# A gated delta rule and six local attention layers on one core: input stage written out as one sequence, output stage moved into the next block

## What is computed

```python
xn = _layernorm(x)
x  = x + gated_delta(xn) + local_layers(xn)      # both read xn alone
# gated_delta, 6 heads, keys 128 wide, values 32 wide
q = conv_silu(xn @ q_w.T); k = conv_silu(xn @ k_w.T); v = conv_silu(xn @ v_w.T)
# per token: S = S*exp(g); S += k (v - k S) beta; o = q S      (q, k scaled to length one)
out = (rms_norm(o) * norm_weight * silu(xn @ g_w.T)) @ o_w.T
# local_layers, six times: h += attn(shift(h)) @ Wo ; h += ffn(shift(h))
```

## Time and profile before

| | before |
|---|---|
| median of 3 runs | 2648.12 us (2646.16 to 2655.34) |
| the profiled execution, own time | 2652.6 us |
| its span | 2650.8 us |
| delta inputs, loop and tail | 24.5 to 178.3 us |
| chunks | 178.3 to 523.6 us |
| delta outputs | 524.8 to 558.8 us |
| local layers' block begins | 560.1 us |

### The profile page before, as it was taken

The page is one execution under the profiler, slowest core; times in us unless marked ns, Lnnn a source line. Parts: engine busy times, 40 slices in busy tenths (PEclk is TensorE's granted clock), DMA queues, the critical chain, the costliest instruction groups (busy, mean ns, idle before and its releaser), DMA issues. The chain is left out here.

```text
span 2650.8 us, 101393 instructions
## 1 busy us (share of the span) xinstructions
PE 2397.2 (90%) x42655; PEld 1589.1 (60%) x42655; DVE 1882.7 (71%) x3765; ACT 1358.9 (51%) x2430; POOL 1557.3 (59%) x2926
## 2 busy tenths in 40 slices
PE   6856999769999999999999999999999997799976
PEld 1224888645666666666666666666666664345544
DVE  6853554337888888888888888888888883576615
ACT  4731332215666556666666666666666663245532
POOL 0024565238877787778777877787777772122330
PEclk9966999959999999999999999999999998889977
DMA  1001111031211122122212221222111110100000
GB/s 36 0 5 30 31 29 30 17 128 50 58 50 52 55 68 69 50 66 60 75 49 63 58 77 50 66 61 78 50 44 45 47 49 26 28 3 4 4 1 16
DMA packets 99663, 118.03 MB, mean 45 GB/s; under 512 B 41342, under 2 KB 57742, under 8 KB 98446
## 3 DMA queue, kind: packets, MB, share of 16 engines
q1 hardware_dynamic: 99214, 111.58, 15.4%
HBM read 29.47 MB, written 7.34 MB: 14 GB/s over the span
## 5 line engine op out<-in xcount | busy, mean ns | idle before, releaser
L1768 POOL TENSOR_TENSOR l_rot_a<-l_rot_a,l_rot_b 128x512 f32<-128x512 f32 x384 | 482.1, 1275 | 214.7 <-DVE l_rot_b L1617 214.5
L1255 PE MATMUL l_A<-l_wts,l_H 128*128 128x512 f32 x768 | 399.5, 603 | 16.5 <-DMA l_maskb<-in_l_mask 10.2
L1777 POOL TENSOR_TENSOR l_qk<-l_rot_a,l_rn 128x512 f32<-128x512 f32 x384 | 388.3, 1043 | 21.5 <-POOLq L1815 21.5
L1611 DVE TENSOR_TENSOR l_rot_a<-l_A,l_tab 128x512 f32<-128x512 f32 x384 | 259.2, 675 | 179.8 <-ACT l_sq L1484 159.1
L1490 ACT ACTIVATE l_pT<-l_T 128x512 f32<-128x512 f32 x192 | 106.6, 595 | 426.3 <-PE l_T L1301 426.3
L1484 ACT ACTIVATE l_sq<-l_A 128x512 f32<-128x512 f32 x384 | 229.2, 597 | 122.5 <-PE l_A L1255 120.1
L1617 DVE TENSOR_TENSOR l_rot_b<-l_A,l_tab 128x512 f32<-128x512 f32 x384 | 261.0, 680 | 0.0
L1621 DVE TENSOR_REDUCE l_ss<-l_sq 128x8 f32<-128x512 f32 x384 | 259.4, 676 | 0.0
L1354 PE MATMUL l_T<-ident,l_qk 128*128 128x128 f32 x1536 | 207.6, 278 | 18.5 <-POOL l_qk L1777 12.0
L1354 PEld LDWEIGHTS l_T<-ident,l_qk 128*128 128x128 f32 x1536 | 173.3, 141 | 83.1 <-issue 58.5
L1360 PEld LDWEIGHTS l_T<-l_oT,l_wts 128*128 128x128 f32 x1536 | 186.3, 192 | 30.8 <-issue 22.1
(11 more groups left out here) (357 smaller groups left out, 5154.6 us busy)
## 6 DMA issues: line engine op xcount, KB each, us to landing
l_vw<-l_vn SPq DMA_DIRECT2D x384, 128.0 KB
l_vw<-l_vn SPq DMA_DIRECT2D x360, 64.0 KB
l_wts<-in_l_wts SPq DMA_DIRECT2D x18, 650.0 KB, 5.0
c_lower_out<-c_amt SPq DMA_DIRECT2D x16, 384.0 KB, 3.2
l_tab<-in_l_tables SPq DMA_DIRECT2D x6, 1024.0 KB, 5.4
l_wts<-in_l_wts SPq DMA_DIRECT2D x6, 635.5 KB, 4.7
c_inv<-c_bx SPq DMA_DIRECT2D x96, 8.0 KB
result<-x SPq DMA_DIRECT2D x4, 256.0 KB
```

What stands on the lines that cost most here:

```text
L1255: pe.matmul(A[j % 2][:], cols(m), w_of(m)[:, C_QKV + 512 * j:C_QKV + 512 * j + 512], start=True, stop=True).then_inc(pq_done, 1)
L1611: dve.tensor_tensor(rot_a[p][:, j, :].rearrange("p (a d) -> p a d", d=DH), src.rearrange("p (a d) -> p a d", d=DH), table[:, a, t:t + 1, : ...
L1768: pool.tensor_tensor(rot_a[m % 2][:, j, :], rot_a[m % 2][:, j, :], rot_b[:, j, :], ALU.add).then_inc(rot_rdy, 1)
L1777: pool.tensor_tensor(qk[:, j, :].rearrange("p (a d) -> p a d", d=DH), rot_a[p][:, j, :].rearrange("p (a d) -> p a d", d=DH), rn[p][:, 8 * ...
```

## The change

Four functions are touched.

- `delta_inputs`: the loop over two sequences is written out as 28 blocks. Of the tail, the 16 small projections `rates` (12 columns, `d_small`) stand behind PE's first block, five of the eight gate pairs (`gates`) stand between blocks, the log decay chain is on POOL, DVE takes two reciprocals behind its block 3, and the first sequence's norms are turned and rooted while the second sequence is being made. The second sequence's roots are on DVE behind the loop. Constants and cleared buffers of the chunks are made here (`Kept`).
- `delta_chunks`: DVE begins with `sums(0)`; the memsets and the reduction are gone; POOL scales the gates chunk by chunk (`scale_gate`).
- `delta_outputs` is gone as a block. Its work stands in `local_layers`: ahead of PE's first projection, with `x` added on DVE in slot -1.
- `local_layers`: SP asks for the first two weight parts and the tables ahead of the other parts and of the mask, with semaphores of their own; `vw` is cleared on POOL; POOL makes the tables of layer 0 ahead of the slots and those of layer 1 in slots 2 to 5; `gl` and `u` lie in the gates' buffer.

```diff
@@ delta_inputs, tensor
+            for i in range(BLOCKS):
+                b, f = divmod(i, NBLK)
+                project(i)
+                if i == 0:
+                    rates()
+                if f >= 2:
+                    sum_squares(b, f - 2)
+                if i == NBLK:
+                    pe.wait_ge(ld_rdy, 1)
+                    turn_norms(0)
...
+                if i in Z_AT:
+                    gates(Z_AT[i])
+            pe.wait_ge(ssq_rdy[0], 1)
+            turn_norms(1)
+            pe.wait_ge(conv_rdy, BLOCKS - 1)
+            for q in range(Z_LOOP, Z_PAIRS):
+                gates(q)
@@ delta_inputs, scalar
+            last_tap(0)
+            act.wait_ge(ab_done, 1)
+            act.activation(zab[:].rearrange("p t h -> p (t h)"), zab_ps, ACT.Copy).then_inc(ab_rdy, 1)
+            last_tap(1)
+            act.activation(a_log[:], a_log[:], ACT.Exp)
+            act.wait_ge(gate_step, 4)
+            act.activation(beta[:], beta[:], ACT.Exp, scale=-1.0)
+            act.activation(e1[:], s1[:], ACT.Exp, scale=-1.0).then_inc(exp_rdy, 1)
@@ delta_inputs, vector
+                if i == 3:
+                    dve.wait_ge(gate_step, 6)
+                    dve.reciprocal(s2[:], s2[:])
+                    dve.reciprocal(beta[:], beta[:]).then_inc(inv_rdy, 1)
+                if i == NBLK + 2:
+                    keep_turned(0)
+            keep_turned(1)
+            dve.wait_ge(ssq_rdy[1], 1)
+            rsqrt(dve, roots_of(1), ssq[1][:], rs_tmp[1][:], 0.0, 1e-6, rinv_step[1], 0, tick["dve"])
@@ delta_chunks, vector and gpsimd
+            sums(0)
             dve.tensor_tensor(gain[:], beta[:], r_k, ALU.mult).then_inc(small_rdy, 1)
-            for b in range(BATCH):
-                dve.memset(state[b][:], 0.0)
...
-            pool.tensor_tensor(gates, gates, r_q, ALU.mult).then_inc(scaled, 1)
...
                 if has(s - 1):
+                    scale_gate(s - 1)
                     gated(s - 1)
@@ local_layers, sync
-            for part in range(4):
-                weights(0, part)
+            sp.dma_start(o_wo, dram["d_wo"]).then_inc(o_ld, 16)
...
+            weights(0, 0)
+            weights(0, 1)
             tables(0)
+            sp.dma_start(x[:], dram["x"].rearrange("(t p) d -> p t d", p=P)).then_inc(x_ld, 16)
+            weights(0, 2)
+            weights(0, 3)
@@ local_layers, tensor
+            def turn_delta(w):
+                if w >= 2:
+                    pe.wait_ge(o_oT_rdy, w - 1)
...
+            def project_delta(w):
+                if w == 0:
+                    pe.wait_ge(wo_rdy, len(VB))
+                pe.wait_ge(o_oT_rdy, w + 1)
...
             pe.wait_ge(h0_rdy, 9)
-            pe.wait_ge(const_ld, 16)
+            turn_delta(0)
+            turn_delta(1)
+            for w in range(OUT_UNITS):
+                project_delta(w)
@@ local_layers, project_v
+                if m == 0:
+                    pe.wait_ge(w_ld[0], w_need(0))
+                    pe.wait_ge(o_x_rdy, NT)
@@ local_layers, vector
+                if n == -1:
+                    dve.wait_ge(x_ld, 16)
+                    dve.wait_ge(rs_step, RSQRT_STEPS)
+                    for t in range(NT):
+                        add_delta(t)
@@ local_layers, gpsimd
-            for layer in range(2):
-                for a in range(4):
-                    table(layer, a)
+            for p in range(2):
+                last = pool.memset(vw[p][:], 0.0)
...
+            for a in range(4):
+                table(0, a)
...
-                if n >= NT and 2 <= t < 6 and layer < DEPTH:
+                if n >= 0 and 2 <= t < 6 and layer < DEPTH:
                     table(layer, t - 2)
```

More of the change, by code:

```diff
@@ L127, in _, with gated_delta @@
             act.wait_ge(xnT_rdy, NT // GT)
-def gated_delta(nc, x, xn, ident, identb, dram, load_inputs):
+@dataclass
+class Kept:
+    tri: object
+    causal: object
+    blocks: object
+    second: object
+    eye: object
+    state: list
+    invT: list
+    u4: object
+    xd: object
+    upper: object
+def gated_delta(nc, x, xn, gate, ident, identb, dram, load_inputs):
     with ExitStack() as ctx:
@@ L136, in gated_delta @@
         vT = sb("vT", [P, len(VB), BATCH * SEQ])
-        gate = sb("gate", [P, NT, VD])
         beta = sb("beta", [P, NT, GH])
@@ L188, with delta_inputs @@
 SERIES = range(15, 1, -2)
-GATE_G = 13 + len(SERIES)
+W_LOADS = 16 * 9
 AMT = 4
 WIDE = 4
-def delta_inputs(nc, ident, xnT, qT, kT, vT, gate, beta, rinv, decay, weights):
+def delta_inputs(nc, ident, xnT, qT, kT, vT, gate, beta, rinv, decay, weights, kept):
     beta, logdecay = beta
@@ L340, in _, with last_tap @@
-            act.wait_ge(gate_step, 3)
-            act.activation(e1[:], s1[:], ACT.Exp, scale=-1.0).then_inc(act_step, 1)
+            def last_tap(i):
+                b, f = divmod(i, NBLK)
+                m = rows(f)
+                act.wait_ge(proj_done, i + 1)
+                if i >= 2:
+                    act.wait_ge(silu_rdy, i - 1)
+                act.activation(conv[i % 2][0:m, :], proj[i % 2][0:m, :], ACT.Copy, scale=w_conv[0:m, f, KCONV - 1:KCONV])\
+                   .then_inc(raw_rdy, 1)
@@ new lines, in keep_gates, with keep_norms @@
+            def keep_gates(q):
+                act.wait_ge(z_done, q + 1)
+                act.activation(gate[:, 2 * q:2 * q + 2, :].rearrange("p t d -> p (t d)"), gate_bank(q)[:, 0:2 * VD], ACT.Silu)\
+                   .then_inc(z_rdy, 1)
+            def keep_norms(b):
+                act.wait_ge(norm_done, 2 * GH * (b + 1))
+                for c in range(2):
+                    last = act.activation(ssqT[:, b, 512 * c:512 * c + 512], norms[c][0:2 * GH, :], ACT.Copy)
+                last.then_inc(norm_rdy, 1)
@@ L342, in _ @@
+            for q in range(Z_LOOP, Z_PAIRS):
+                keep_gates(q)
             act.wait_ge(sums_done, 1)
-            act.activation(decay[:].rearrange("p a t h -> p (a t h)"), sums[:, 0:3 * SMALL], ACT.Exp).then_inc(act_step, 1)
-            act.wait_ge(act_step, 4)
+            act.wait_ge(ssq_rdy[1], 1)
+            act.activation(decay[:].rearrange("p a t h -> p (a t h)"), sums, ACT.Exp).then_inc(decay_rdy, 1)
+            act.wait_ge(decay_rdy, 1)
+            act.wait_ge(z_rdy, Z_PAIRS)
@@ L409, in _ @@
[L409 to L419 removed]
+            pool.wait_ge(w_ld, W_LOADS)
@@ new lines, in _ @@
+            rsqrt(pool, roots_of(0), ssq[0][:], rs_tmp[0][:], 0.0, 1e-6, rinv_step[0], 0, tick["pool"])
+            pool.wait_ge(rinv_step[0], RSQRT_STEPS)
+            pool.tensor_scalar(rinv[:, 0:GH, 0:TB], rinv[:, 0:GH, 0:TB], float(HK) ** -0.5, None, ALU.mult).then_inc(rinv_rdy, 1)
+            for buffer in (*kept.state, *kept.invT, kept.u4, kept.xd, kept.upper):
+                last = pool.memset(buffer[:], 0.0)
+            last.then_inc(cleared, 1)
+            pool.wait_ge(cleared, 1)
@@ L421, in delta_chunks @@
+def delta_chunks(nc, spare, ident, identb, kqT, vT, gate, beta, logdecay, rinv, decay, kept, dram):
     with ExitStack() as ctx:
         sb, ps, sem = buffers(nc, ctx)
-        tri = sb("c_tri", [P, 3, P])
-        causal = sb("c_causal", [P, P], BF16)
-        blocks = sb("c_blocks", [P, P], BF16)
-        second = sb("c_second", [P, 2])
+        tri, causal, second, eye = kept.tri, kept.causal, kept.second, kept.eye
+        state, invT, u4, xd, upper = kept.state, kept.invT, kept.u4, kept.xd, kept.upper
```

502 lines of the change are left out of this document (235 added, 267 removed).

## The result

| | before | changed |
|---|---|---|
| median, same chip | 2649.63 us (2646.16 to 2655.34, 4 runs) | 2604.48 us (2600.08 to 2610.83, 4 runs) |
| the profiled execution, own time / span | 2652.6 / 2650.8 us | 2605.12 / 2603.4 us |

The ratio is 0.9829, 95% interval 0.9802 to 0.9857: 45 us faster. The forecast was 2613 us, with a range of 2594 to 2627. Borders are starts of instructions, and for the loop its end; the maximum (`l_mx`) is the first step of a tile's softmax on DVE, and the last column is the forecast's term for the stretch.

A forecast was written before the change was run, and what follows sets the result against it. It took DVE to bound the inputs' loop and PE at half clock the outputs, with waits at stage borders. Terms -9.7 - 10.7 - 17.8 - 1.3 + 4.2 = -35.3 us gave 2613 us, range 2594 to 2627.

The forecast's parts named there:

- its own case: Main forecast for the whole kernel, given 58%: 2604 to 2623 us, inputs gaining 4 to 18, tables costing 0 to 4.9.
- signs of being wrong: Full clock in the outputs, DVE taps idling in the loop after block 4, or chunks of another period than before.
- Loop's start: Inputs' loop, first blocks: small projections, ACT's exponentials, PE's line and reciprocals together cost +14.3 us, from +7 to +17.
- as PE is at half here I take 9: Inputs' loop behind block 0: the 32 small passes take 9 us on PE, between bounds of 3.9 and 11.5.
- Now ACT also loads the exponential's table: Inputs' loop before DVE's block 2: an added table load and three small exponentials on ACT cost 1.28 + 0.7 us.
- Border: Inputs' loop between the two sequences: DVE's idle time there goes, -6.6 us, less 0.3 for a copy.
- Tail: Behind the inputs' loop: 6.8 us of DVE work and a 2.0 us barrier replace 26.5 us, -17.7.
- chunks' setup: Start of the chunks' block: `sums(0)` comes first, so the first product waits 1.1 us instead of 11.9, -10.7.
- outputs: Output products at half clock within the local layers' block, transfers hidden behind PE: first rotary step 17.8 us sooner.
- roots: Local layers' start: POOL's roots follow the last rotated half after about 8.5 us instead of 9.9, -1.3.
- Tables: Layer 1's four tables in slots 2 to 5, where POOL is the bound: +4.2 us.
- The rival at the full clock: Outputs keep the full clock and take 11 us instead of 27.7: 17 us less, 2596 us; chance 20%.

The follow-up runs named there:

- The experiment on the rates: Changed kernel with the 32 small passes moved on PE behind block 2, ACT's copy and exponentials behind blocks 2 and 3, reciprocals behind block 6: 2605.68 us, ratio 0.9851.
- the side-by-side kernels: On one chip: the changed kernel as it is, 2603.99 us, and the same with spare transposes at two places in the local layers' block, 2591.91 us.
- the kernel with two fills: Changed kernel plus ten unread PE transposes behind the turned xn and ten behind the first two output turns, none at the chunks' end: 2591.91 us, ratio 0.9782.
- the one with tile 0 between the outputs: Changed kernel with tile 0's four local products and ACT's squares placed between the last five of eight output units: 2591.19 us, ratio 0.9798.
- the kernel before with fills: Kernel before plus ten spare transposes at the chunks' end and 32 in place of PE's wait for the output weights: 2638.06 us, ratio 0.995.

## Why the prediction was right, point by point

The number was right, and by luck as well as by its argument. Of the forecast's three steps for the loop, the start was off by 7.3 us and the pace by 5.4 in one direction, the border by 8.3 in the other, so that the loop's end came out within 4.6. And the median of 2604.48 lies at the edge of the 2604 to 2623 that the forecast gave its own case. One of its own signs of being wrong came true: DVE's taps idle in the loop behind block 4, at blocks 15 and 16. Of the other signs, block 2 stood at 39.9 and not at 50, the loop's end at 155 and not at 160, and the chunks' block at 163 and not at 169.

**Loop's start: mis-sized.** The step "as PE is at half here I take 9" priced the small projections. They took 3.87 us in the first profile, most of it at the full clock, and 6.84 at half: the bound of 11.5, from passes with 128 columns moving, doesn't hold for these with 12. The step "Now ACT also loads the exponential's table" was false: there is no such load in the trace, the changed kernel has fewer loads than before, and block 2 starts 4.9 us behind block 1, not 7.1. Nor does the one load take longer than its 1.28 us, as the next activation starts 0.01 us behind it. On the other side, from block 2 to block 4 it took 14.8 us and not the 12.0 of the forecast. Block 4 stood 7.0 us later, and 6.6 to 9.9 in nine profiles with this start, not 14.3. The experiment on the rates shows that pricing single passes was the wrong kind of sum: the idle time is shared among blocks 1 to 5.

**Loop's pace: a term that was missing.** The semaphore increments, in the diff for all to see, were not priced. 84 times 0.074 us are 6.2 us, shown by putting them back.

**Border: the step failed.** "At the border of the sequences the loop no longer drains", priced at -6.6. DVE's waits of 6.6 us went, but others of 8.3 came, as the work moved there stood ahead of the product that DVE waited for. The forecast had looked at the queue of the engine that gives the work up, not at the one that takes it. Moving it by two blocks and more gave 6.8 us against this profile, 5.7 on average. The half clock at that place is a part of it that the forecast had not reckoned with either.

**Tail, chunks' setup, outputs, roots: right,** -18.4, -10.9, -17.9 and -1.6 us. (The tail's working, 17 instructions at 0.29 and 0.1 us, gives 6.6 us and not 6.8.) `scale_gate` cost nothing that the chunks would show: from their first product to the last gate product it takes 330.6 to 335.5 us in twelve profiles with it, 332.8 and 331.9 in two without. The additions to `x` fell into DVE's waits, as argued: behind them (550.07 to 554.28) DVE still waits 2.04 us for ACT. This was not tested by itself.

**Tables: right in mechanism, 2.2 to 3.0 us and not 4.2.** The profile of before, long in these slots, made it look like nothing.

**The clock: right, with its reason.** The outputs ran at half the clock. The rival at the full clock, with 20%, was argued down because PE is "busy for only half the time" ahead of them, and that idle time was indeed the cause: PE was busy 3.03 of the last 5.5 us where the clock fell, and 5.21 where it stayed. The rival's price was wrong, 11 us for outputs that take 15.7, from passes of 0.12 us that take 0.2 here. The Trainium skill, TensorE: Matmul & The Clock Gate, section "Why this matters for your kernels", warns of long idle gaps between bursts of matmuls. The runs agree that idle time costs throughput, 12.1 us by the side-by-side kernels, but not that it takes one long gap: the longest here, 2.9 us, is also in the kernel with two fills, which kept the clock. The same page of the Trainium skill, section "What's actually happening", says that activity releases the throttle; the outputs, 27.3 us without a break at 0.51, don't bear it out for these products.

**What is left.** The 4.4 us behind tile 8 belong to no part of the change: from the maximum of tile 0 to that of tile 95 it takes 1594.7 to 1601.1 us in the thirteen other profiles, the changed kernel's 1596.1 among them, and 1600.4 in that of before. So these 4.4 of the profiles' 47.4 us lie within the scatter between executions.

## What to carry to other kernels

Work moved under a bound engine is hidden only if it stands behind what that engine waits for, on the engine that takes it: look at the line ahead of that product, and move the work by a few blocks. Look at the granted clock of a stretch that PE bounds before reckoning with its length: here twenty spare transposes gave 12 us, a quarter of what the whole rewrite gave, and 42 gave 11 us in the kernel before. Count the table loads in the trace before pricing one. Read a cost of 3 us from several executions: one profile of before hid it.

## What the runs showed of the hardware

- The same 88 passes of 128 columns ran for 27.3 us at granted 0.51 and did not raise the clock, and ran for 15.7 us at 1.00 without lowering it. In the changed kernel and in the one with tile 0 between the outputs it rose 3.8 and 2 us behind the start of the first product with 512 columns moving (534.73 and 516.51). In the kernel before with fills, where PE had idled 10.3 us ahead of such products, it rose only at the third pair, 12 us behind the first. But no such product is needed: in the kernel before it rose right behind 16 passes of transposes, with none of 512 columns, and fell again while PE idled:

```profile
560.00:564.00 4.00, 3.65 (x16) 3.28 (x16) 3.04 (x4) 1.92 (x4) 0.00 (x0) 0.50 0.71 223
564.00:567.60 3.60, 0.00 (x0) 0.00 (x0) 3.21 (x7) 0.45 (x1) 0.00 (x0) 0.97 1.01 415
```

  What decides stays open.
- An output pass of 128 columns takes 0.35 us at half the clock (8 in 2.80) and 0.205 at the full clock (8 in 1.64): less than twice.
- At the head of the loop the granted clock reads 1.00 while a pass of 512 columns takes 0.84 us. At a granted 0.50 a pass takes the same, and some 0.5 at the full clock. The windows of the kernel before:

```profile
28.00:32.00 4.00, 4.00 (x6) 1.35 (x4) 1.40 (x2) 1.11 (x1) 0.00 (x0) 1.00 0.00 0
```

  The duration of a pass tells more than the clock's row there.
- A semaphore increment ahead of each tap costs DVE 0.074 us (1.351 us a tap with it, 1.277 without).
